# Keys ahead of queries, lengths and rows turned early: one change to a fused vision tower on one core

## The reference, cut to what matters

```python
q = q / (norm(q) + EPS); k = k / (norm(k) + EPS)      # heads of 64
alpha = sigmoid(h @ alpha_w + alpha_b)                # one per key feature
beta = sigmoid(h @ beta_w + beta_b)                   # one per head
def step(s, inp):                                     # s: 64 x 64 per head
    qt, kt, vt, at, bt = inp
    s = s * at[..., None]
    u = einsum('bhd,bhdv->bhv', kt, s)
    s = s + bt * (kt[..., None] * (vt - u)[..., None, :])
    return s, einsum('bhdv,bhd->bhv', s, qt)
```

## Time and profile before

| | us |
|---|---|
| median of 3 runs | 832.8 |
| lowest, highest | 829.75, 835.26 |
| the profiled execution | 832.5 |
| its span, first to last instruction | 830.4 |
| PE busy in the span | 696.5 |
| DVE busy in the span | 360.0 |
| ACT, POOL busy in the span | 247.9, 158.0 |

### The profile page before, as it was taken

The page is one execution under the profiler, slowest core; times in us unless marked ns, Lnnn a source line. Parts: engine busy times, 40 slices in busy tenths (PEclk is TensorE's granted clock), DMA queues, the critical chain, the costliest instruction groups (busy, mean ns, idle before and its releaser), DMA issues. The chain is left out here.

```text
span 830.4 us, 20092 instructions
## 1 busy us (share of the span) xinstructions
PE 696.5 (84%) x9130; PEld 519.2 (63%) x9130; DVE 360.0 (43%) x529; ACT 247.9 (30%) x467; POOL 158.0 (19%) x134
## 2 busy tenths in 40 slices
PE   8867157992999994879999999976679979999997
PEld 5546156782888883664466666655369966655554
DVE  0486954550111111251457666775944780421220
ACT  0461123120323220322034545424624443111033
POOL 9001001003000004400045555651013310000000
PEclk9978658995999996878999999999669999999999
DMA  9000000007998833000000002000000041000001
GB/s 343 23 1 1 0 2 2 1 2 279 355 336 297 331 127 114 1 1 19 1 21 23 23 22 73 4 3 2 0 2 5 4 185 72 1 1 0 1 1 39
DMA packets 19365, 56.39 MB, mean 68 GB/s; under 512 B 4177, under 2 KB 12241, under 8 KB 14929
## 3 DMA queue, kind: packets, MB, share of 16 engines
q1 hardware_dynamic: 18512, 53.01, 17.5%
q0 software_dynamic: 768, 2.10, 0.7%
HBM read 49.58 MB, written 5.52 MB: 66 GB/s over the span
## 5 line engine op out<-in xcount | busy, mean ns | idle before, releaser
L1325 PEld LDWEIGHTS PS<-arena 64*49 64x49 f32 x3584 | 63.0, 124 | 32.7 <-issue 20.4
L1325 PE MATMUL PS<-arena 64*49 64x48 f32 (+2 forms) x3584 | 71.4, 229 | 7.7 <-DVE arena L1555 5.3
L1284 PE MATMUL PS<-Y,arena 128*128 128x392 f32 x192 | 76.1, 527 | 0.4 <-DVE beta_tok L1508 0.4
L1533 DVE COPY_PREDICATED arena<-msk,PS 128x768 f32<-128x768 int32 x32 | 55.9, 1746 | 37.6 <-PE PS L1325 37.5
L216 PE MATMUL PS<-fill 128*128 128x256 bf16 x530 | 67.4, 281 | 3.3 <-DVE fill L1436 2.1
L216 PEld LDWEIGHTS PS<-fill 128*128 128x128 bf16 x530 | 51.9, 101 | 15.5 <-DVE fill L1436 2.1
L1234 PEld LDWEIGHTS PS<-arena 128*128 128x128 f32 x448 | 54.4, 199 | 2.4 <-issue 1.0
L1234 PE MATMUL PS<-arena 128*128 128x128 f32 x448 | 54.8, 283 | 1.2 <-DVE arena L1484 1.2
L972 POOL TENSOR_TENSOR arena<-arena 128x384 f32<-128x384 f32 (+1 forms) x32 | 38.6, 1206 | 87.7 <-PE PS L1325 87.6
L1032 ACT ACTIVATE arena<-PS,arena 128x128 f32<-128x128 f32 x112 | 31.9, 368 | 69.1 <-PE PS L1234 69.1
L366 POOL TENSOR_TENSOR arena<-arena,work 128x512 f32<-128x512 f32 x20 | 25.4, 1270 | 136.1 <-DVE work L650 136.0
(11 more groups left out here) (206 smaller groups left out, 1141.0 us busy)
## 6 DMA issues: line engine op xcount, KB each, us to landing
arena<-in_moe_w SPq DMA_DIRECT2D x28, 1024.0 KB, 6.4
arena<-in_qka_w SPq DMA_DIRECT2D x8, 384.0 KB, 3.1
arena<-in_patches SPq DMA_DIRECT2D x3, 784.0 KB, 6.4
arena<-in_ff_w SPq DMA_DIRECT2D x1, 2048.0 KB, 7.7
arena<-in_ffn_w SPq DMA_DIRECT2D x2, 1024.0 KB, 13.3
by_expert<-arena SPq DMA_DIRECT2D x1, 1792.0 KB, 13.4
arena<-in_moe_b SPq DMA_DIRECT2D x14, 128.0 KB, 6.8
arena<-by_expert SPq DMA_DIRECT2D x14, 128.0 KB, 2.5
```

Of the source, the lines that this page charges most:

```text
L1284: m = nc.tensor.matmul(bank(i % 3), GW[g % 2][:, k, u // 2], half(Y[:, k], u % 2), start=(k == 0), stop=(k == KT - 1))
L1325: m = nc.tensor.matmul(o, K[r, b, :], v, start=True, stop=True)
L1533: nc.vector.copy_predicated(dst, mk, src).then_inc(lv_kept, 1)
```

## The change

- `KQ_SET` has the axes c, batch, token: all first keys lie ahead of all queries, and a row of tokens is contiguous. `later_moving` becomes two instructions, one for keys and one for queries, for levels 4, 8 and 16, and stays one for levels 2 and 32.
- `first_keys` on POOL is gone; `first_moving` on DVE multiplies keys and queries in one instruction (its input is the view `FIRST_SET`, the plain keys and the queries).
- The copies of level 8 (unit 4) go from one masked copy on DVE to six rectangles on ACT.
- In the second layer the sums are turned at the end of step 26 (`TURNED`) through bank 3, with ACT's roots there too; DVE's lengths stand behind step 27, the columns on PE behind step 29, DVE's copy of them behind step 30. POOL's clear stands behind step 26. After the last unit PE turns row groups 0 to 3 having waited for ACT's copies up to the one before the last, and waits for the last, of level 32, only ahead of group 4.
- XS has 14 slots. SP loads the rows of tiles 0 to 2, expert 1, the rows of tiles 3 to 13, then experts 2 and 3; its wait for turned rows is gone.
- `delta0` is called through the new, smaller functions in the order it had.

```diff
-        XS = at(4096, 3 * D).rearrange("p (s n) -> p s n", s=3)
+        XS = at(19648, NT * D).rearrange("p (s n) -> p s n", s=NT)
...
-        KQ_SET = [at(S0 + 4 * BT * i + BT, 2 * BT).rearrange("p (b t c) -> p b t c", b=B, c=2) for i in range(NSET)]
+        KQ_SET = [at(S0 + 4 * BT * i + BT, 2 * BT).rearrange("p (c b t) -> p c b t", c=2, b=B) for i in range(NSET)]
+        FIRST_SET = [at(S0 + 4 * BT * i, 3 * BT).rearrange("p (x n) -> p x n", x=3)[:, 0:3:2] for i in range(NSET)]
...
         N_STEPS = 7 * (FT // 2) + LAG
+        TURNED = 7 * (FT // 2 - 1) + LAG + 2
...
-        kept_by_dve = place_of(lambda g, k: k <= 4)
-        kept_by_act = place_of(lambda g, k: k >= 5)
+        kept_by_dve = place_of(lambda g, k: k <= 3)
+        kept_by_act = place_of(lambda g, k: k >= 4)
...
             for j in range(3):
                 load_rows(j)
-            for j in range(1, NW):
+            load_expert(1)
+            for j in range(3, NT):
+                load_rows(j)
+            for j in range(2, NW):
                 load_expert(j)
             for j in range(NT):
                 sp.wait_ge(y_kept, j + 1)
                 sp.dma_start(answers[j * P:(j + 1) * P, :], YS[:, j % 2]).then_inc(stored[j % 2], 16)
-                if j + 3 < NT:
-                    sp.wait_ge(xt_mm, j + 1)
-                    load_rows(j + 3)
...
-            def first_keys(g):
-
-                pool.wait_ge(g_kept, piece[g, 5] + 1)
-                nc.gpsimd.tensor_tensor(KQ_SET[g % NSET][..., 0], K_SET[g % NSET], DECAY_SET[g % NSET], ALU.mult) \
-                    .then_inc(lv_first, 1)
...
+                if tau == TURNED:
+                    pool.wait_ge(lv_mm, unit[FT - NSET + 1, 6] + 1)
+                    delta1.pool_clear(pool)
...
+                    if k == 4:
+                        for n in range(3):
+                            m = nc.scalar.activation(dst[o:o + 9 + 16 * n, :, :, 9 + 16 * n:17 + 16 * n],
+                                                     src[o:o + 9 + 16 * n, :, :, 8 * n:8 * n + 8], ACT.Copy)
...
+                if tau == TURNED:
+                    delta1.act_roots(act, 3)
...
+                if tau == TURNED:
+                    pe.wait_ge(ss_kept, 1)
+                    delta1.pe_sums(pe, 3)
+                if tau == TURNED + 3:
+                    delta1.wait(pe, "rooted", 2)
+                    delta1.pe_cols(pe, 3)
 
             pe.wait_ge(lv_kept, len(kept_by_dve))
-            pe.wait_ge(lv_act, len(kept_by_act))
-            pe.wait_ge(ss_kept, 1)
-            delta1.pe_in(pe)
-            delta1.wait(pe, "lengths", delta1.n_lengths + 1)
+            pe.wait_ge(lv_act, len(kept_by_act) - 1)
+            for g in range(delta1.NGI):
+                if g == 3:
+                    delta1.wait(pe, "lengths", delta1.n_lengths + 1)
+                if g == 4:
+                    pe.wait_ge(lv_act, len(kept_by_act))
+                delta1.pe_rows(pe, g)
...
-            def first_queries(g):
+            def first_moving(g):
 
                 dve.wait_ge(g_kept, piece[g, 5] + 1)
-                q_ = KQ_SET[g % NSET][..., 1]
-                nc.vector.tensor_tensor(q_, q_, DECAY_SET[g % NSET], ALU.mult).then_inc(lv_moving, 1)
+                nc.vector.tensor_tensor(KQ_SET[g % NSET].rearrange("p c b t -> p c (b t)"), FIRST_SET[g % NSET],
+                                        over(DECAY_SET[g % NSET].rearrange("p b t -> p (b t)"), 2), ALU.mult) \
+                    .then_inc(lv_moving, 1)
...
-                    v = blocks_kq(moving, q)[:, :, :, 1]
-                    end = blocks(ends, q)[:, :, :, 0, q - 1:q].broadcast_to([P, B, 48 // h, 2 * q])
-                nc.vector.tensor_tensor(v, v, end, ALU.mult).then_inc(lv_moving, 1)
+                    end = blocks(ends, q)[:, :, :, 0, q - 1:q].broadcast_to([P, B, 48 // h, q])
+                    for cc in range(2):
+                        v = blocks(moving[:, cc], q)[:, :, :, 1]
+                        m = nc.vector.tensor_tensor(v, v, end, ALU.mult)
+                    m.then_inc(lv_moving, 1)
...
-            dve.wait_ge(g_sum, FT)
-            nc.vector.tensor_copy(ss[:, 0:HB, 0:T], bank(3)).then_inc(ss_kept, 1)
+                if tau == TURNED - 1:
+                    dve.wait_ge(g_sum, FT)
+                    nc.vector.tensor_copy(ss[:, 0:HB, 0:T], bank(3)).then_inc(ss_kept, 1)
+                if tau == TURNED + 1:
+                    delta1.dve_lengths(dve)
+                if tau == TURNED + 4:
+                    delta1.dve_cols(dve, 3)
```

More of the change, by code:

```diff
@@ L58 @@
 MASK, _at = {}, 0
-for _name, _n in [("strict", T), ("upto", T), ("diag", T)] + [(f"level{h}", NSLOT) for h in LEVELS[:4]]:
+for _name, _n in [("strict", T), ("upto", T), ("diag", T)] + [(f"level{h}", NSLOT) for h in LEVELS[:3]]:
     MASK[_name] = (_at, _n)
@@ L412, in dve_solve, with dve_cols @@
                         self.wait(dve, "lengths", i)
-                    if i == len(steps) - 1:
-                        self.wait(dve, "cols_turned", 1)
                     step().then_inc(self.s["lengths"], 1)
-                self.wait(dve, "lengths", len(steps))
+            def dve_cols(self, dve, bank_):
+                self.wait(dve, "cols_turned", 1)
+                nc.vector.tensor_copy(
+                    sys_cols[0:self.S].rearrange("p k c t -> p (k c) t"),
+                    PS[0:self.S, bank_, 0:2 * P].rearrange("p (n t) -> p n t", t=TP)[:, :, 0:2 * BL]) \
+                    .then_inc(self.s["lengths"], 1)
+            def dve_solve(self, dve):
+                S = self.S
+                self.wait(dve, "lengths", self.n_lengths + 1)
                 bt = sys_cols[0:S, 0].rearrange("p c t -> p t c").unsqueeze(3)
@@ L700, in tower @@
         stored = [sem(f"answers_stored{i}") for i in range(2)]
-        xs_loaded = [sem(f"rows_loaded{i}") for i in range(3)]
+        xs_loaded = [sem(f"rows_loaded{i}") for i in range(NT)]
         xt_mm, xt_kept, up_mm, gelu, down_mm, y_kept, y_turned, moe_res = [
@@ L709, in tower @@
         g_mm, g_copied, g_kept, g_sum, ss_kept = [sem("g_" + x) for x in ("mm", "copied", "kept", "summed", "sums_kept")]
-        lv_mm, lv_kept, lv_act, lv_moving, lv_keys, lv_ends, lv_first = [
-            sem("level_" + x) for x in ("mm", "kept", "kept_act", "moving", "keys", "ends", "first_keys")]
+        lv_mm, lv_kept, lv_act, lv_moving, lv_keys, lv_ends = [
+            sem("level_" + x) for x in ("mm", "kept", "kept_act", "moving", "keys", "ends")]
         delta1 = Delta(delta0, H1, A1, PT1, W1, U1, D1, OT1, NS1, TS1, 0.0, 1e-6, 1e-6,
@@ L1188, in _ @@
             pe.wait_ge(pairs0_kept, 8)
-            delta0.pe_in(pe)
+            delta0.pe_sums(pe, 4)
+            for g in range(delta0.NGI):
+                if g == 3:
+                    delta0.pe_cols(pe, 5)
+                delta0.pe_rows(pe, g)
             delta0.wait(pe, "rows_in", delta0.NGI)
@@ L1319, in small @@
                             if k == 0:
-                                v, o = moving[r, b, :, 1], o[:, pair * T:(pair + 1) * T]
+                                v, o = moving[r, 1, b], o[:, pair * T:(pair + 1) * T]
                             else:
-                                v = later(moving[r, b], LEVELS[k - 1])
+                                v = later(moving[r, :, b], LEVELS[k - 1])
                                 o = o[:, pair * 64:pair * 64 + 64].rearrange("p (c s) -> p c s", c=2)
@@ L1457, in _ @@
                         .then_inc(pairs0_kept, 1)
+            delta0.dve_lengths(dve)
+            delta0.dve_cols(dve, 5)
             delta0.dve_solve(dve)
@@ L1549, in later_moving @@
                 if h == 32:
[L1550 to L1555 removed]
+                    v = moving[:, :, :, 33:T]
+                    nc.vector.tensor_tensor(v, v, over(ends[:, :, 32:33].broadcast_to([P, B, 16]), 2),
+                                            ALU.mult).then_inc(lv_moving, 1)
+                elif h == 2:
+                    v = moving[:, :, :, 2:T:2]
+                    nc.vector.tensor_tensor(v, v, over(ends[:, :, 1:T:2], 2), ALU.mult).then_inc(lv_moving, 1)
+                else:
+                    end = blocks(ends, q)[:, :, :, 0, q - 1:q].broadcast_to([P, B, 48 // h, q])
[3 more added lines that the diff above has]
+                    m.then_inc(lv_moving, 1)
             for tau in range(N_STEPS):
@@ L1657, in _constants @@
     mput("diag", lambda i, t: i == t, range(T))
-    for h in LEVELS[:4]:
+    for h in LEVELS[:3]:
         toks = [t for t in range(1, T) if (t - 1) // h % 2]
```

94 lines of the change are left out of this document (42 added, 52 removed).

## The result

The changed kernel takes 810.24 us (median of 4 runs, 808.44 to 810.98) against 834.03 us for the kernel before beside it: a ratio of 0.9718, with a 95% interval of 0.9674 to 0.9762. The profiled execution took 810.12 us around a span of 808.3 us; against the 832.5 us of before that is 22.4 us less, where 15.3 were forecast. All ratios here are of runs taken side by side and can differ by 0.3% from the quotient of the two medians; single runs of 1250.37 us (the turn alone) and 2524.49 us (a kernel before) are left out of them.

A forecast was written before the change was run, and what follows sets the result against it. PE's rate was taken to bound the second layer's level products until its next operand is late. The sum was 832.5 - 8.2 (levels) - 6.0 (into the solve) - 1.1 (experts) = 817.2 us, range 811 to 828.

The forecast's parts named there:

- The products and the join: Level products: levels 1, 2, 4 save 1.56 us of PE per pair, joined product waits 0.62; half cycle 17.4 us.
- the lock's rival: POOL's level 16 multiplication gets in ahead of the join, which takes 2.5 us, not 1.83: 822.6 us, chance 0.14.
- S + 1.99: S is the start of a pair's level 0 product; POOL's level 16 multiplication can start about 1.99 us later.
- Opening -1.4 and half cycles -4.8: Second layer's levels: 1.4 us less from 412.36 to 430.98 us, then 4.8 less over five half cycles.
- The end of the levels: From 522.84 us to the last product at 562.41, where one pair's chain sets the pace: -2.0 us.
- +0.2: Last pair's level 8 step: 3.6 us against 3.39 before, with ACT copying and DVE making lengths; no gain.
- Into the solve: From the last level product to the solve's first step: -6.0 us, between -3.7 and -6.5.
- The experts: Expert tiles: row waits go (-5.6), expert 2 comes late (+3.3), clock (+1.2): -1.1 us, between -4.1 and +2.8.
- Stride as no cause: Level products: the new layout doesn't shorten them, so the 12.5 us of PE time stay: 830 us, chance 0.08.
- the slower case: Levels: products unchanged and the join at 2.5 us, so the join becomes the bound: 835.3 us, chance 0.05.
- a starved expert 2: Experts: row loads take 8.0 us ahead of expert 2, full clock loss: 821.1 us, or 824 if half longer; chance 0.10.
- a join of 1.5 us with loads at 415 GB/s: Rival of more gain than forecast, from a quicker join and quicker row loads: 812 us, chance 0.05.

The follow-up runs named there:

- the turn alone: The kernel before with only sums, roots, lengths, columns and the first row groups of the second layer early: 827.15 us, ratio 0.9931.
- rows 6.9: The kernel before with only the token row loads changed (14 XS slots, rows 3 to 13 behind expert 1): 825.6 us, ratio 0.9915.
- layout 3.3: The kernel before with only keys ahead of queries and the later multiplications split; first keys on POOL, level 8 on DVE: 829.22 us, ratio 0.9959.

## Why the prediction came out short

The span fell by 22.1 us. Against the 15.3 forecast that is 6.8 more: 3.7 in the norms and beta, for which the sum had no term, 1.9 in the experts, 1.5 on the way into the solve and 0.5 ahead of the experts and behind the solve; the levels gave 0.8 less. By the runs of single edits the largest miss is that of the rows, 6.9 us where 1.1 had been forecast.

**The products and the join: right, by two errors that cancel.** It had 1.56 us less of PE per pair, and 0.62 us of wait; it is 1.9 us less (17.44 - 0.98 against 18.37) and 0.98 of wait. Levels 8, 16 and 32 became shorter too, by 0.19, 0.17 and 0.09, where it had left them at their old times, and level 4 came to 0.97 and not 0.90. The half cycle is 17.44 us, it said 17.4. The wait is larger as the lock's rival came true at half its price: with POOL ahead the join takes 2.12 us instead of 1.76, with DVE ahead it would be the 0.6 us forecast (at 443.53 us PE waits 0.32, behind a level 8 product that took 0.31 longer). The prediction had POOL's start at S + 1.99, DVE's at S + 2.03, and let DVE win. DVE did start at S + 2.00, but POOL at S + 1.79, as it needs only the level 8 product, and that was the 0.19 us shorter. So the two errors are one: where levels 0 and 8 took 1.61 us together, in five cycles, POOL was first, and where they took 1.92, DVE was. Opening -1.4 and half cycles -4.8 were measured at -1.4 and -4.8.

**The end of the levels: mis-sized.** -2.0 were predicted, -1.2 measured in the profile (39.57 us from 522.84 to 562.41 before; 38.37 from 509.34 to 547.71 after). From the level 0 to the level 8 product of the last pair 0.67 us were gained where the sum has 1.23. This is what POOL and DVE did there:

```profile
535.19 3.03 POOL L362 MEMSET arena<- 128x3400 f32 x2
```

```profile
538.85 1.57 DVE L1582 TENSOR_TENSOR arena<-arena 128x384 f32<-128x384 f32 x2
```

The prediction let POOL's clear hide: "the level 8 keys come 0.7 us later and still before DVE's operand". They do come later, from 538.16 to 540.01 us, and so run beside DVE's two halves, which take 1.57 us where they took 1.05 at 535.14. The product waited 2.20 us, in the kernel before 1.64. No run moves the clear alone, so this is read from the overlap.

**Level 8: the number right, the reason wrong.** "+0.2" at the end was right: 3.64 us from that product to the next, where it was 3.39 before. But "moving level 8 to ACT thus gains nothing" failed as a statement on the edit: without it the levels are 7 to 8 us longer. It pays for the room that the join and the lengths take on DVE. Only its difference to the kernel before is nothing.

**Into the solve: mis-sized.** -6.0 predicted, -7.5 measured. The steps were right (48 row transposes in 5.93 us for 6.0); the idle matmuls behind the last product cost 0.5 us and not 1.05, DVE's last group and the diagonal 0.7 and not 0.9, and the low clock, for which 0.5 us had been set aside, did not come. (Its price was off too: eight groups at that clock took 5.56 us, where the pace of the first twelve transposes gives 4.0, so it costs some 1.5 us and not 2.8.) PE's stretch while it turns rows, for the 0.57 of the earlier trace rows:

```profile
550.00:556.00 6.00, 6.00 (x46) 5.39 (x45) 4.62 (x14) 2.30 (x2) 0.00 (x0) 1.00 0.02 5
```

**The experts: the step that failed.** -1.1 was predicted; it is -3.0 between the two profiles, and -4.8 between the means of three profiles each. Three terms of the sum were mis-sized. The first is the waits: it took the 5.6 us that PE's list names. From the third up product to the last, however, the kernel before takes 7.2 us more than eleven times the 7.245 us of a tile without wait, and 6.7 to 8.9 in five other profiles that have its rows: tile 2 to tile 3, say, took 8.60 us where PE shows a wait of 1.14, that is 1.36 over 7.245; tile 4 to tile 5 took 7.72 with a wait of 0.26. Both are 0.2 us more than PE's idle time. PEld's list of waits has most of it:

```profile
PEld PS L1224 <- DMA arena<-by_expert: 7.0, 7, 1.7
```

The second is the pause for expert 2: 3.3 us were predicted, and in nine profiles with this order it was 1.8 to 2.6 us. All loads together went at 394 GB/s from 203 to 217 us, and at that rate the 1.44 MB of rows take 3.7 us and not 5.3. The third is the clock, for which 1.2 us stood as a mean. It is one of two: the third up product took 3.84 us in five of the nine profiles and 5.46 or 5.47 in the other four. In the profile the three come to -7.2 + 2.5 + 1.7 = -3.0, where the sum had -5.6 + 3.3 + 1.2.

**What no term could hold.** 3.7 us of the profile's difference lie in the norms and beta. The granted clock there, before and after, at the same norm:

```profile
338.00:344.00 6.00, 4.63 (x27) 4.11 (x27) 3.06 (x4) 1.28 (x3) 2.94 (x1) 0.72 0.00 0
```

```profile
334.20:340.20 6.00, 4.65 (x42) 4.37 (x43) 3.36 (x5) 2.30 (x5) 3.18 (x1) 1.00 0.00 0
```

The second kernel does the same work at the full clock (2.4 GHz), the first fell to the lower level (1.2 GHz) for a part. Both further executions of the kernel before have the shorter form (49.9 and 49.0 us). So the profile that the sum was made against was a long one in this place. The prediction looked at its total alone, which was near the median, and took no correction. Part of these 3.7 us is luck, and whether the change has a part in them is open, as said above. That the medians differ by 22 to 24 us all the same is not fully accounted for: rows 6.9, layout 3.3 and turn 5.3 alone make 15.5, and the join and level 8 were only measured by taking them out of the whole (4 and 10 us longer in device time, and these overlap).

**The rivals.** Stride as no cause, the slower case and a starved expert 2 did not come; the lock came at 0.35 us in five of eight joins. Two of their sums were off by 1 us: row loads half as long again as 8.0 us give 825 and not 824, and a join of 1.5 us with loads at 415 GB/s gives 813 and not 812.

## What to carry to other kernels

Price a wait by what the whole loop loses against its unhindered period, not by the list of one engine's idle time. When one instruction is split in two under a shared port, look for a long instruction of the other engine that fits into the gap; and when an edit seems to gain nothing, ask whether it makes room for another one of the same change. Where an operand is late by 1 us, look first for work of the waiting engine that can be put in front of it: moving one sum by a line shortened the levels by 3 us here, without touching the engine that was late. And before a sum is made against one profile, profile the kernel again: its norms took 51.3, 49.9 and 49.0 us in three executions.

## What the runs showed that was not expected

- The time of a float32 product of 64 records and 48 columns depends on how its moving operand is spread: 1.54 us at steps of 16 bytes, 0.90 at steps of 8 (level 1) and for pairs at steps of 4 (level 2). But 0.97 for fours (level 4) is more than for pairs, so the spread is not all. Halving the step shortened the products of levels 16 and 32 too (1.23 to 1.06, 1.14 to 1.05), whose moving operand lay in runs already.
- Who is first at the shared port is decided by 0.1 to 0.2 us, and most cycles repeat it: the same join took 2.10 to 2.12 us in five cycles and 1.76 or 1.77 in three.
- A POOL instruction that comes second is recorded with its waiting time: 2.23 us at 441.80 for a form that takes 0.68.
- The granted clock falls at varying places of the same work: the norms took 51.3, 49.9 and 49.0 us in three executions of the kernel before, and filling the idle stretch ahead of them with 50 matmuls moved the fall and did not shorten them (52.3 us).
